# Convolved attention on one Trainium2 core: a new order of TensorE's work within a step

## The reference

```python
attn  = einsum('bhqd,bhkd->bhqk', q, k) * hd**-0.5        # 8 batches, 16 heads, 256 x 256
attn0 = where(causal_mask, 0.0, attn)
attn  = conv3x3(attn0, kernels[b, h])                     # one 3 x 3 kernel for each batch and head
attn  = where(causal_mask, -inf, attn)
out   = softmax(attn) @ v
return out_heads_joined @ proj_W + proj_b
```

## Time and profile before

| what | value |
|---|---|
| three executions | 2223.65, 2229.43, 2230.05 us; median 2229.43 |
| the profiled execution, its own time | 2223.91 us |
| its span, first to last instruction | 2222.2 us |
| PE busy in the span | 1821.4 us, 82% |
| VectorE, ScalarE, GpSimd busy | 1031.4, 957.6, 743.3 us |
| granted TensorE clock over the span | 0.907 |

### The profile page before, as it was taken

One profiled execution on the slowest core, in us unless ns is written; L12 is line 12 of the kernel. 1 busy time (PEld: TensorE's weight loads), 2 busy tenths in 40 slices (PEclk: granted clock), 3 DMA queues, 4 the chain that ended last, 5 costly groups with the idle time before them and its releaser, 6 DMA issues. The chain is left out here.

```text
span 2222.2 us, 40660 instructions
## 1 busy us (share of the span) xinstructions
PE 1821.4 (82%) x13563; PEld 1308.2 (59%) x13585; DVE 1031.4 (46%) x3515; ACT 957.6 (43%) x2468; POOL 743.3 (33%) x904
## 2 busy tenths in 40 slices
PE   6849999989598888887499988984893988887594
PEld 5737766666344444444389965644782866555493
DVE  2552224653455555553400058865346546984323
ACT  3633221432345555555333346754442435775220
POOL 1012202110355555542011054410645737641233
PEclk9959999999699999999689999995895998999697
DMA  4313212000311111100289944416676685433394
GB/s 146 115 52 133 64 41 94 19 20 8 54 35 32 34 36 33 34 20 9 84 322 355 332 132 103 114 51 254 197 150 252 183 150 136 108 93 123 98 352 128
DMA packets 171224, 260.81 MB, mean 117 GB/s; under 512 B 23056, under 2 KB 136592, under 8 KB 166928
## 3 DMA queue, kind: packets, MB, share of 16 engines
q1 hardware_dynamic: 150960, 208.65, 28.9%
q0 software_dynamic: 16704, 45.64, 9.3%
q10 hardware_dynamic: 3360, 3.93, 0.7%
HBM read 181.46 MB, written 37.75 MB: 99 GB/s over the span
## 5 line engine op out<-in xcount | busy, mean ns | idle before, releaser
L508 POOL DMA_INDIRECT weights_xg<-xn_rows,token_of x197 | 189.2, 961 | 418.9 <-DVE token_of L698 168.5
L1893 ACT ACTIVATE heads_probsT<-heads_ps_e 128x512 f32<-128x512 f32 x256 | 148.1, 597 | 69.2 <-PE heads_ps_e L1736 62.4
L1047 PE MATMUL experts_ps_g<-weights_w,experts_xT 128*128 x504 | 136.4, 395 | 1.7 <-issue 0.7
L1070 PE MATMUL experts_ps_y<-weights_w,experts_hT 128*128 (+1 forms) x486 | 134.1, 385 | 1.2 <-DVE experts_y L1132 1.2
L2224 PE MATMUL heads_ps_t<-ident,heads_mixes 128*128 128x128 f32 x576 | 103.5, 288 | 32.0 <-ACT heads_probsT L2318 19.5
L2307 ACT ACTIVATE heads_mixes<-heads_mixes,heads_least 128x256 f32<-128x256 f32 x288 | 118.4, 497 | 17.9 <-DVE heads_least L2464 17.9
L1712 PE MATMUL heads_ps_m<-heads_stackK,heads_stackQ 96*128 96x256 bf16 x512 | 100.1, 280 | 23.6 <-DMA heads_stackQ<-heads_q_pieces 9.4
L1104 ACT ACTIVATE experts_silu<-experts_ps_g 128x128 f32<-128x128 f32 (+1 forms) x165 | 53.0, 321 | 153.2 <-PE experts_ps_u L1052 80.3
L2201 PE MATMUL heads_ps_c<-heads_S,heads_band 32*32 32x512 f32 x3072 | 112.8, 606 | 0.4 <-DVE heads_least L2464 0.4
L2318 ACT COPY heads_probsT<-heads_ps_t 128x240 f32<-128x240 f32 x256 | 84.8, 362 | 64.4 <-PE heads_ps_t L2224 62.7
L2224 PEld LDWEIGHTS heads_ps_t<-ident,heads_mixes 128*128 128x128 f32 x576 | 60.1, 141 | 79.3 <-issue 70.1
(11 more groups left out here) (443 smaller groups left out, 4319.3 us busy)
## 6 DMA issues: line engine op xcount, KB each, us to landing
experts_w<-in_experts_dram SPq DMA_DIRECT2D x23, 2180.0 KB, 10.4
weights_w<-in_experts_dram SPq DMA_DIRECT2D x32, 768.0 KB, 5.7
weights_w<-in_experts_dram SPq DMA_DIRECT2D x14, 1536.0 KB, 18.7
y_rows<-experts_y SPq DMA_DIRECT2D x125, 128.0 KB, 1.8
heads_stackK<-heads_k_pieces SPq DMA_DIRECT2D x192, 64.0 KB, 2.6
heads_stackQ<-heads_q_pieces SPq DMA_DIRECT2D x192, 64.0 KB, 3.1
weights_w<-in_experts_dram SPq DMA_DIRECT2D x8, 1088.0 KB, 5.5
xn_rows<-xn SPq DMA_DIRECT2D x4, 2048.0 KB, 7.6
```

The costliest lines, as they stand in the source:

```text
L508: pool.indirect_dma_start(self.xg[:, u, :], None, xn_dram, bass.IndirectOffsetOnAxis(ap=tb.token_of[:, j:j + 1], axis=0)).then_inc(self.x_ ...
L1047: last = pe.matmul(ps_g[:, j % 2, 0:2 * F], xT[:, j % 2, c, :], w[:, bass.ds(at_slot(at[j], c * 2 * F), 2 * F)], start=(c == 0), stop=(c = ...
L1070: last = pe.matmul(ps_y[:, j % BY, 0:D], hT[0:m, j % 2, f * P:(f + 1) * P], w[0:m, bass.ds(at_slot(at[j], DC * 2 * F + f * D), D)], start= ...
L1893: act.activation(probsT[:, h, :], ps_e[:, h % 2, :], ACT.Exp).then_inc(exped, 1)
```

## The change

It changes the order in which PE, DVE and ACT issue a step's work, the banks of `ps_s` that go with it, and the counts that the waits name. No instruction of work is added or removed.

- PE, step n: mix of n-2; taps 0, 1, 2 of n; last scores of n+1; then the nine turns of n-1 with other work between them: after turn 1 window 8's convolution of n, after turn 3 scores 2 of n+1, after turn 5 scores 3 of n+1 and in odd steps the query and key projection, after turn 6 in odd steps the value projection; turn back of n-2; scores 0 and 1 of n+2. (The turns count from 0.)
- Window 8 moves from the first to the fourth place in `ORDER`, which sets the order of the maxima, exponentials, turns and copies.
- The scores' banks become 0, 1, 0, 1; last scores go to bank 0 and window 8's convolution to bank 1.
- DVE, step n: maskings 0 and 1 of n+1; maxima 0 and 1; masking last; maxima 2 to 4; masking 2; maxima 5 and 6; masking 3; maxima 7 and 8; finish of n-2; take.
- ACT places the values after copy 7 instead of copy 4.

The core of the diff (left out: the same change of order before the loops, and the new counts in `drop_masked`, `drop_masked_last` and `row_max`, which follow from it):

```diff
-    ORDER = (8, 0, 4, 1, 5, 2, 6, 3, 7)
+    ORDER = (0, 4, 1, 8, 5, 2, 6, 3, 7)
+    AT = [ORDER.index(k) for k in range(NW)]
...
             def score(n, j):
-                u, bank = n // 2, (0, 1, 1, 0)[j]
+                u, bank = n // 2, (0, 1, 0, 1)[j]
...
-                if j < 2 and n > 0:
-                    pe.wait_ge(masked, ENTRIES * (n - 1) + GH + j)
-                if j == 0 and n >= 3 and n % 2 == 1:
-                    pe.wait_ge(qk_taken, min((n + 5) // 2, ROUNDS))
-                if j == 1 and n >= 3 and n % 2 == 1:
-                    pe.wait_ge(v_placed, (n + 1) // 2)
+                    if n > 0:
+                        pe.wait_ge(masked, ENTRIES * (n - 1) + 4)
+                    if n >= 3 and n % 2 == 1:
+                        pe.wait_ge(qk_taken, min((n + 5) // 2, ROUNDS))
+                if j == 1:
+                    if n > 0:
+                        pe.wait_ge(masked, ENTRIES * n)
+                    if n >= 3 and n % 2 == 1:
+                        pe.wait_ge(v_placed, (n + 1) // 2)
                 if j == 2:
-                    pe.wait_ge(masked, ENTRIES * n + 2)
+                    pe.wait_ge(masked, ENTRIES * n + 3)
                 if j == 3:
-                    pe.wait_ge(masked, ENTRIES * n + 1)
                     if n > 0:
-                        pe.wait_ge(maxed, NW * (n - 1) + 1)
+                        pe.wait_ge(maxed, NW * (n - 1) + AT[8] + 1)
+                    else:
+                        pe.wait_ge(masked, 2)
...
             def score_last(n):
...
-                pe.wait_ge(masked, ENTRIES * n + 3)
+                pe.wait_ge(masked, ENTRIES * n + 1)
...
             def convolve_last(n):
-                pe.wait_ge(masked, min(ENTRIES * (n + 1) + 1, ENTRIES * QUADS))
+                pe.wait_ge(masked, min(ENTRIES * (n + 1) + 2, ENTRIES * QUADS))
...
             for n in range(QUADS + 2):
                 ahead, back = n + 1 < QUADS, 1 <= n <= QUADS
-                if ahead:
-                    score(n + 1, 0)
-                    score(n + 1, 1)
-                if n < QUADS:
-                    convolve(n, 0)
-                    convolve_last(n)
-                if ahead:
-                    score(n + 1, 2)
-                if n < QUADS:
-                    convolve(n, 1)
-                if ahead:
-                    score(n + 1, 3)
-                    score_last(n + 1)
-                if n < QUADS:
-                    convolve(n, 2)
                 if n >= 2:
                     mix(n - 2)
+                if n < QUADS:
+                    for dk in range(TAPS):
+                        convolve(n, dk)
+                if ahead:
+                    score_last(n + 1)
                 for k in range(NW):
                     if back:
                         turn(n - 1, k)
-                    if k == 2 and n % 2 == 1 and n // 2 + 3 < ROUNDS:
-                        pe.wait_ge(masked, ENTRIES * (n + 1) + GH)
+                    if k == 1 and n < QUADS:
+                        convolve_last(n)
+                    if k == 3 and ahead:
+                        score(n + 1, 2)
+                    if k == 5 and ahead:
+                        score(n + 1, 3)
+                    if k == 5 and n % 2 == 1 and n // 2 + 3 < ROUNDS:
+                        pe.wait_ge(masked, ENTRIES * (n + 1) + 4)
                         project_query_key(n // 2 + 3, 0)
-                    if k == 3 and n % 2 == 1 and n // 2 + 1 < ROUNDS:
+                    if k == 6 and n % 2 == 1 and n // 2 + 1 < ROUNDS:
                         pe.wait_ge(masked, ENTRIES * (n + 2))
                         project_value(n // 2 + 1, 1)
                 if n >= 2:
                     turn_back(n - 2)
+                if n + 2 < QUADS:
+                    score(n + 2, 0)
+                    score(n + 2, 1)
...
         @block.scalar
...
-                    if k == 4 and n % 2 == 1 and n // 2 + 1 < ROUNDS:
+                    if k == 7 and n % 2 == 1 and n // 2 + 1 < ROUNDS:
                         place_values(n // 2 + 1)
...
         @block.vector
...
-            for n in range(-1, QUADS + 2):
-                if n + 1 < QUADS:
+            for n in range(QUADS + 2):
+                ahead = n + 1 < QUADS
+                if ahead:
                     drop_masked(n + 1, 0)
                     drop_masked(n + 1, 1)
-                if 0 <= n < QUADS:
-                    row_max(n, 0)
-                if n + 1 < QUADS:
-                    drop_masked(n + 1, 2)
-                    drop_masked(n + 1, 3)
-                    drop_masked_last(n + 1)
-                if 0 <= n < QUADS:
-                    for k in range(1, NW):
+                for k in range(NW):
+                    if n < QUADS:
                         row_max(n, k)
+                    if k == 1 and ahead:
+                        drop_masked_last(n + 1)
+                    if k == 4 and ahead:
+                        drop_masked(n + 1, 2)
+                    if k == 6 and ahead:
+                        drop_masked(n + 1, 3)
                 if n >= 2:
                     finish(n - 2)
```

More of the change, by code:

```diff
@@ L2183, in score_last @@
                 r = u % STACKS
-                pe.wait_ge(masked, ENTRIES * n + 3)
+                pe.wait_ge(masked, ENTRIES * n + 1)
                 for j in range(GH):
                     h = GH * (n % 2) + j
-                    last = pe.matmul(ps_s[LANE * j:LANE * (j + 1), 1, 0:SEQ], stackQ[:, r, h, 2 * P:QW],
+                    last = pe.matmul(ps_s[LANE * j:LANE * (j + 1), 0, 0:SEQ], stackQ[:, r, h, 2 * P:QW],
                                      stackK[:, r, h, :], start=True, stop=True, skip_group_check=True)
@@ L2207, in convolve_last @@
             def convolve_last(n):
-                pe.wait_ge(masked, min(ENTRIES * (n + 1) + 1, ENTRIES * QUADS))
+                pe.wait_ge(masked, min(ENTRIES * (n + 1) + 2, ENTRIES * QUADS))
                 for dk in range(TAPS):
-                    last = pe.matmul(ps_s[:, 0, 0:SEQ], band_last[:, n % 2, dk, :, :].rearrange("p j m -> p (j m)"),
+                    last = pe.matmul(ps_s[:, 1, 0:SEQ], band_last[:, n % 2, dk, :, :].rearrange("p j m -> p (j m)"),
                                      S_last[:, n % 2, dk:dk + SEQ], start=(dk == 0), stop=(dk == TAPS - 1),
@@ L2255, in _ @@
             pe.wait_ge(v_placed, 1)
-            for j in range(GH):
-                score(0, j)
+            score(0, 0)
+            score(0, 1)
             score_last(0)
+            score(0, 2)
+            score(0, 3)
+            score(1, 0)
+            score(1, 1)
             pe.wait_ge(constants, 1)
@@ L2438, in drop_masked @@
             def drop_masked(n, j):
-                bank = (0, 1, 1, 0)[j]
-                v.wait_ge(scored, ENTRIES * n + j + 1)
+                v.wait_ge(scored, ENTRIES * n + (1, 2, 4, 5)[j])
                 if j == 0 and n >= 2:
@@ L2443, in drop_masked @@
                 v.tensor_tensor(S[:, n % 2, j, :, 1:SEQ + 1],
-                                ps_s[:, bank, :].rearrange("p (c n) -> p c n", c=2), keep[:, :, :], ALU.mult)\
+                                ps_s[:, j % 2, :].rearrange("p (c n) -> p c n", c=2), keep[:, :, :], ALU.mult)\
                     .then_inc(masked, 1)
             def drop_masked_last(n):
-                v.wait_ge(scored, ENTRIES * (n + 1))
+                v.wait_ge(scored, ENTRIES * n + 3)
                 if n >= 2:
                     v.wait_ge(convolved_last, n - 1)
-                v.tensor_tensor(S_last[:, n % 2, 1:SEQ + 1], ps_s[:, 1, 0:SEQ], keep_last[:, :], ALU.mult)\
+                v.tensor_tensor(S_last[:, n % 2, 1:SEQ + 1], ps_s[:, 0, 0:SEQ], keep_last[:, :], ALU.mult)\
                     .then_inc(masked, 1)
@@ L2455, in row_max @@
                 at = ORDER[k]
-                if k == 0:
+                if k == 0 and n >= 2:
+                    v.wait_ge(turned, NW * (n - 1))
+                if at == NW - 1:
                     v.wait_ge(convolved_last, n + 1)
-                    if n >= 2:
-                        v.wait_ge(turned, NW * (n - 1))
-                    got = ps_s[:, 0, 0:SEQ]
+                    got = ps_s[:, 1, 0:SEQ]
                 else:
-                    v.wait_ge(convolved, GROUPS * n + (k - 1) // 2 + 1)
+                    v.wait_ge(convolved, GROUPS * n + at % GROUPS + 1)
                     got = ps_c[:, at % GROUPS, at // GROUPS * SEQ:(at // GROUPS + 1) * SEQ]
```

9 lines of the change are left out of this document (7 added, 2 removed).

## The result

The changed kernel took 2197.86 us in the median of 4 runs (2191.51 to 2199.72), the kernel before 2229.74 (2223.65 to 2231.49). The ratio is 0.9857 [0.983, 0.9884]: 32 us faster, where 39 were predicted. The profiled execution took 2198.34 us, with a span of 2196.6; from its first to its last instruction the stage went from 458.2 to 427.8 us, 30.4 less, and the rest of the span is 4.8 us longer than in the profile of before.

What follows compares the result with a forecast made beforehand. The prediction took PE in order, its work plus the turns' round trips, as the bound. Gains of 22.2 (even steps), 12.9 (odd) and 4.2 (steps 27, 29, 31) make 39 us: 2229.4 - 39 = 2190 us, range 2172 to 2212.

Steps and rivals of the forecast that it cites:

- The even step: Even-numbered steps of the stage on PE: predicted 10.28 us against 11.76 before, a gain of 1.48 each.
- Taps: Three taps in a row on PE: 3.15 to 3.47 us, middle 3.31 taken, so grouping costs 0.09.
- the first rival: Taps in one mode flow on, each 0.88 after the last: three take 2.83 us, total 2175; chance 0.12.
- Two windows and window 8's convolution: Start of the turns on PE: two windows at 0.24 us each, then the convolution 1.40, together 1.88.
- The round trips: Turn, copy, free of a bank, 0.95 us each: three plus 0.24 make 3.09 from window three to turn back.
- The mix: Mix moved ahead of the taps: its copy is ready early, so the second window's 0.70 us wait goes.
- The odd step: Odd-numbered steps on PE: predicted 14.55 us against 15.54, gain 0.99, with 2.06 from turn back to scores staying whole.
- The sum: Stage total: 15 x 1.48 = 22.2, 13 x 0.99 = 12.9 and 4.2 for steps 27, 29, 31; 39 us.
- Steps 27 and 29: Late odd steps without query projection or its wait: predicted 11.15 us, gain taken as the even steps', 1.4 each.
- Rival 2: Work inserted among the turns comes on top of the round trips, nothing hidden: time as before, about 2230; chance 0.09.
- Rival 3: VectorE's chain from window 8's convolution to fourth masking, at double length, delays PE: 24 us slower, 2253; chance 0.07.
- VectorE's and GpSimd's new waits: VectorE's maxima and maskings and GpSimd's bands now wait for window 8's convolution: hidden, cost taken at nothing.

## Why the prediction was right, and where its 7 us went

- *The even step.* 10.28 predicted, 10.22 measured. Taps 3.31, measured 3.33 to 3.34: grouping costs 0.1, and the first rival's 2.83 did not come. It had the starts right: in the group of 96 at 784.63 the second and third tap (matmuls 33 and 65) start 0.88 and 1.76 after the first. But the next kind of work starts 1.57 after the third tap, not 1.07, so what the group saves inside it loses at its end. My 3.31 was the middle of two bounds, and that it came so near is in part luck. Two windows and window 8's convolution 1.88, measured 1.79. The round trips 3.09, measured 3.09.
- *The mix.* The second window starts 0.28 after the first (788.19 and 788.47); the wait is gone, as the run with the mix behind shows from the other side.
- *The odd step.* 14.55 predicted, 14.43 measured (769.20 to 783.63, mix to mix). The 2.06 us from turn back to scores stayed, 2.05. But I priced it as idle time alone. What it does to the clock behind it was not in the sum, put at nothing without a word: six falls of 1.55, 9.3 us.
- *The sum.* From one window 8's convolution to the next, without the falls, the steps gain 39.9 us, where I had 39. The parts differ: the first two intervals gained 2.4, where I had 1.0 for step 1; steps 27 and 29 gained 0.5 each instead of 1.4. Ahead of the first of these convolutions the stage lost 4.0 and behind the last it gained 4.0. Less 9.3, that is 30.6 for the stage, and 30.4 was measured. The profiled executions lie 25.6 apart, since the rest of the span, where nothing was changed, took 4.8 more; the 32 is of medians. So the falls' 9.3 account for the missing 7 only to within some us.
- *Steps 27 and 29.* They took 11.97, where the working had 11.15. PE waits there for VectorE's fourth masking, ahead of the value projection, since no query projection stands between; before had no such wait:

```profile
955.69 1.16 PE L2155 MATMUL heads_ps_s<-layer_w,xnT 128*128 128x128 f32 x8 [0.64 <-DVE heads_S L2450]
```

- *The rivals.* Rival 2 was wrong, but the run with the work ahead of the turns is what it describes: time as before. Rival 3 was wrong: in the even and odd steps shown PE does not wait for the third or fourth masking; only steps 27 and 29 have such a wait.
- *VectorE's and GpSimd's new waits* cost nothing, as taken, but for the 0.64 in those two steps.

Open: what decides, from one wait to the next, whether the clock falls. The runs show that the idling is needed for it: with the wait filled, gone or cut to 0.78 us there was no fall. They show that the new order is not needed. That the place of the wait in time decides fits the runs, but is not shown.

## What to carry to other kernels

A latency loop of two buffers (turn, copy, free) is best paid with work that has to be done anyway: put it between the turns, not ahead of them. Matmuls of one shape need not stand together for that: here it cost 0.1 us a step to group them. When a schedule gets denser, look at the waits that stay: each can cost more than its idle time, in the work right behind it, and a short TensorE wait that did no harm at one step length may do so at another.

## What the runs showed of the hardware that was not expected

- A wait of 1.64 us (2.05 from turn back to scores) let TensorE's clock fall to 1.2 GHz behind it in 6 of 12 cases after, in none of 12 before, and in 6 of 12 with the old order made 0.86 us a pair longer (one profiled execution each). With dummy matmuls in the wait it stayed at 2.4 GHz there, and the kernel with more work was 11 us faster.
- Three fp32 taps of sixteen 32 x 32 blocks took 3.33 in a row, 1.07 to 1.09 each apart. In the row the next tap starts after 0.88, sooner than apart, but behind the last one 1.57 pass to the next kind of work, so the row saves nothing.
